# VectorE's order inside a Runge-Kutta stage: operations placed between the two scans that close the stage

## The reference, cut to what matters

```python
def _derivative(q, p, drive, coupling, bias):
    i_couple = jnp.tanh(q) @ coupling.T
    dq = q - q ** 3 / 3.0 - p + drive + i_couple + bias
    dp = EPSILON * (q + ALPHA - BETA * p)
    return (dq, dp)

def _rk4_step(q, p, drive, coupling, bias):
    dq1, dp1 = _derivative(q, p, drive, coupling, bias)
    dq2, dp2 = _derivative(q + 0.5 * DT * dq1, p + 0.5 * DT * dp1, drive, coupling, bias)
    dq3, dp3 = _derivative(q + 0.5 * DT * dq2, p + 0.5 * DT * dp2, drive, coupling, bias)
    dq4, dp4 = _derivative(q + DT * dq3, p + DT * dp3, drive, coupling, bias)
    q_next = q + DT / 6.0 * (dq1 + 2 * dq2 + 2 * dq3 + dq4)
    p_next = p + DT / 6.0 * (dp1 + 2 * dp2 + 2 * dp3 + dp4)
    q_next = jnp.clip(q_next, -CLAMP, CLAMP)
    p_next = jnp.clip(p_next, -CLAMP, CLAMP)
    return (q_next, p_next)
```

## Time and profile before

| what | us |
|---|---|
| median of 3 runs | 5615.42 |
| the profiled execution's own time | 5619.32 |
| its span, first to last instruction | 5617.5 |
| the stretch of the 512 steps in it | 2971.85 |
| VectorE busy in that stretch | 2823.98 |
| TensorE busy in that stretch | 2125.34 |

### The profile page before, as it was taken

One profiled execution on the slowest core, in us unless ns is written; L12 is line 12 of the kernel. 1 busy time (PEld: TensorE's weight loads), 2 busy tenths in 40 slices (PEclk: granted clock), 3 DMA queues, 4 the chain that ended last, 5 costly groups with the idle time before them and its releaser, 6 DMA issues. The chain is left out here.

```text
span 5617.5 us, 214944 instructions
## 1 busy us (share of the span) xinstructions
PE 4455.2 (79%) x79945; PEld 3854.9 (69%) x79945; DVE 4321.5 (77%) x25970; ACT 2307.7 (41%) x10530; POOL 1700.8 (30%) x5981
## 2 busy tenths in 40 slices
PE   6777777777777777777776888599999999969999
PEld 5666666666666666666665666578777787758777
DVE  8999999999999999999996666377777777731123
ACT  3333333333333333333333556255555555432243
POOL 2333333333333333333333322023232323200000
PEclk5555555555555555555556999699999999989999
DMA  1000000000000000000002001222222221131031
GB/s 69 1 1 1 1 1 1 1 1 1 1 1 1 1 1 1 1 1 1 1 1 77 9 24 35 92 65 75 79 94 79 64 94 57 57 120 60 24 112 38
DMA packets 145846, 188.08 MB, mean 33 GB/s; under 512 B 9372, under 2 KB 75492, under 8 KB 145288
## 3 DMA queue, kind: packets, MB, share of 16 engines
q1 hardware_dynamic: 140800, 182.67, 9.7%
q0 software_dynamic: 624, 0.75, 0.1%
q10 hardware_dynamic: 3992, 0.17, 0.0%
HBM read 143.67 MB, written 39.90 MB: 33 GB/s over the span
## 5 line engine op out<-in xcount | busy, mean ns | idle before, releaser
L211 PE MATMUL bank<-tanh_parts,w_lo 128*128 128x4 f16 x32768 | 1208.6, 169 | 845.9 <-ACT tanh_parts L168 845.8
L211 PEld LDWEIGHTS bank<-tanh_parts,w_lo 128*128 128x128 f16 x32768 | 1034.9, 105 | 1029.7 <-ACT tanh_parts L168 1029.2
L168 ACT ACTIVATE tanh_parts<-ys 128x8 f16<-128x8 f32 x4096 | 851.2, 208 | 1902.6 <-DVE ys L306 1902.3
L219 PE MATMUL bank<-tanh_parts,w_hi 128*128 128x8 f16 x32768 | 1206.5, 173 | 1.6 <-issue 1.6
L219 PEld LDWEIGHTS bank<-tanh_parts,w_hi 128*128 128x128 f16 x32768 | 1063.3, 104 | 1.7 <-issue 1.7
L169 ACT ACTIVATE tanh_full<-ys 128x8 f32<-128x8 f32 x4096 | 803.3, 196 | 0.0
L306 DVE TENSOR_TENSOR_SCAN ys<-mix,bank 128x24 f32<-128x24 f32 x4096 | 719.0, 198 | 57.5 <-PE bank L219 3.8
L298 DVE TENSOR_TENSOR tanh_parts<-tanh_full,tanh_parts 128x8 f16<-128x8 f32 x4096 | 689.2, 178 | 0.5 <-ACT tanh_full L169 0.5
L1281 POOL TENSOR_TENSOR t_w_qk<-t_raw_qk,t_w_qk 128x512 fp32r<-128x512 f32 x128 | 168.1, 1335 | 771.4 <-ACT t_w_qk L1445 771.4
L486 PE MATMUL t_bank<-t_x,t_w_qk 128*128 128x512 f32 x1536 | 361.1, 391 | 12.8 <-DVE t_x L1701 12.8
L486 PEld LDWEIGHTS t_bank<-t_x,t_w_qk 128*128 128x128 f32 x1536 | 289.8, 189 | 73.9 <-DVE t_x L1701 13.5
(11 more groups left out here) (238 smaller groups left out, 9545.9 us busy)
## 6 DMA issues: line engine op xcount, KB each, us to landing
t_raw_qk<-L_cond_qkv_w_dram SPq DMA_DIRECT2D x128, 256.0 KB, 3.3
t_raw_vo<-L_cond_qkv_w_dram SPq DMA_DIRECT2D x16, 1024.0 KB, 5.1
t_raw_vo<-L_cond_out_w_dram SPq DMA_DIRECT2D x16, 1024.0 KB, 5.3
n<-t_parts SPq DMA_DIRECT2D x14, 1024.0 KB, 6.6
g_raw<-L_cond_ffn_w_dram SPq DMA_DIRECT2D x8, 1024.0 KB, 9.1
g_x<-n SPq DMA_DIRECT2D x8, 1024.0 KB, 8.6
ada_w<-L_cond_ada_w_dram SPq DMA_DIRECT2D x4, 1536.0 KB, 11.1
t_x<-n SPq DMA_DIRECT2D x6, 1024.0 KB, 7.2
```

What stands on the lines that cost most here:

```text
L168: act.activation(tanh_parts[:, u, at, :, 0], ys[:, s, at, :, 2], ACT.Tanh, scale=1.0 / SCALE).then_inc(s_th, 1)
L211: pe.matmul(sums[:, :, 2], w_lo[:, w_of, k, m * P:(m + 1) * P], tanh_parts[:, u, k, :, 0], start=(m % 2 == 0 and k == 0), stop=False, skip ...
L219: last = pe.matmul(sums[:, :, 1:3], w_hi[:, w_of, k, m * P:(m + 1) * P], tanh_parts[:, u, k], start=False, stop=(m % 2 == 1 and k == C - 1 ...
```

## The change

It does four things, all in VectorE's program:

1. `result` takes a function `between` and runs it between the two scans. In stage 0 the operation `p_1` stands there, in stage 1 the second `known`, in stage 3 the clip of `p`; stage 2 has none.
2. `twice` moves from in front of stage 0's scans to in front of stage 1's. Stage 1's first `known` moves from in front of its `mix` to the stage's start, in front of `cub`. Stage 1's `mix` now stands in front of `p_2`.
3. In stage 0 the first low part stands in front of `cub`.
4. `settle` and the clearing of `s_dve` are gone; the count runs on to the end. With it the loop over steps calls the four stages plainly.

The waits follow: the first scan of stage 0 now waits for `s_mm` and for `s_dve` (the end of `mix`), as stage 3's did and does, and the clip of `p` waits for nothing of its own.

```diff
-            def settle():
-
-                nonlocal n
-                v.wait_ge(s_dve, n)
-                v.sem_clear(s_dve)
-                n = 0
-                marks.clear()
...
-            def result(t, s):
+            def result(t, s, between=None):
...
                                          banks[2 * u + half][:, 0:C // 2 * B * 3], 0.0, ALU.mult, ALU.add).then_inc(s_q, 1)
+                    if half == 0 and between is not None:
+                        between()
...
             def stage_0(t):
...
+                low_part(t, 0, 0)
                 v.wait_ge(s_clip, t + 1)
                 cubed(q[:, :, :])
-                low_part(t, 0, 0)
                 low_part(t, 0, 1)
...
                 based(0, known[:, 0])
-                v.wait_ge(s_rate, t * 3 + 1)
-                own("p_1", stt(ps_[:, 1], rate[:, 0], EPSILON * H, p[:, :, :]))
                 after("base")
-                own("twice", stt(twice[:, :, :], net[:, :, :], 2 * H, q[:, :, :]))
-                result(t, 0)
+
+                def between():
+                    v.wait_ge(s_rate, t * 3 + 1)
+                    own("p_1", stt(ps_[:, 1], rate[:, 0], EPSILON * H, p[:, :, :]))
+                result(t, 0, between)
 
             def stage_1(t):
+                own("known", stt(known[:, 1], rate[:, 0], -EPSILON * H * H, known[:, 0]))
                 v.wait_ge(s_q, t * 2 * STAGES + 4)
...
-                own("known", stt(known[:, 1], rate[:, 0], -EPSILON * H * H, known[:, 0]))
+                after("slope")
+                based(1, known[:, 1])
                 v.wait_ge(s_rate, t * 3 + 2)
                 own("p_2", stt(ps_[:, 2], rate[:, 1], EPSILON * H, p[:, :, :]))
-                after("known")
-                based(1, known[:, 1])
                 v.wait_ge(s_third, t + 1)
                 own("third_1", stt(thirds[:, 1], y1, THIRD, thirds[:, 0]))
                 after("base")
-                own("known", stt(known[:, 2], rate[:, 1], -2 * EPSILON * H * H, twice[:, :, :]))
-                result(t, 1)
+                own("twice", stt(twice[:, :, :], net[:, :, :], 2 * H, q[:, :, :]))
+
+                def between():
+                    after("twice")
+                    own("known", stt(known[:, 2], rate[:, 1], -2 * EPSILON * H * H, twice[:, :, :]))
+                result(t, 1, between)
...
                 based(3, thirds[:, 3])
-                after("moved")
-                v.tensor_scalar(p[:, :, :], p_new[:, :, :], (-CLAMP - SHIFT_P) * SCALE, (CLAMP - SHIFT_P) * SCALE,
-                                ALU.max, ALU.min).then_inc(s_p, 1)
                 after("base")
-                result(t, 3)
-
-            def up_to_stage_2(t):
+
+                def between():
+                    v.tensor_scalar(p[:, :, :], p_new[:, :, :], (-CLAMP - SHIFT_P) * SCALE, (CLAMP - SHIFT_P) * SCALE,
+                                    ALU.max, ALU.min).then_inc(s_p, 1)
+                result(t, 3, between)
...
-                if t + 1 < T:
-                    up_to_stage_2(t + 1)
-                    if t % UNROLL == UNROLL - 1:
-                        settle()
```

More of the change, by code:

```diff
@@ L375, in stage_2 @@
                 own("late", stt(known[:, 3], rate[:, 2], -2 * EPSILON * H * H / 3, thirds[:, 2]))
+                result(t, 2)
             def stage_3(t):
@@ L390, in stage_3 @@
                 based(3, thirds[:, 3])
-                after("moved")
-                v.tensor_scalar(p[:, :, :], p_new[:, :, :], (-CLAMP - SHIFT_P) * SCALE, (CLAMP - SHIFT_P) * SCALE,
-                                ALU.max, ALU.min).then_inc(s_p, 1)
                 after("base")
-                result(t, 3)
-            def up_to_stage_2(t):
+                def between():
+                    v.tensor_scalar(p[:, :, :], p_new[:, :, :], (-CLAMP - SHIFT_P) * SCALE, (CLAMP - SHIFT_P) * SCALE,
+                                    ALU.max, ALU.min).then_inc(s_p, 1)
+                result(t, 3, between)
+            for t in range(T):
                 stage_0(t)
@@ L400, in up_to_stage_2 @@
                 stage_2(t)
-            def from_stage_2(t):
-                result(t, 2)
                 stage_3(t)
[L406 to L409, removed]
-                if t + 1 < T:
-                    up_to_stage_2(t + 1)
-                    if t % UNROLL == UNROLL - 1:
-                        settle()
             v.wait_ge(s_q, T * 2 * STAGES + 2)
```

## The result

The changed kernel takes 5520.49 us, the median of 4 runs (5515.4 to 5520.96); the kernel before took 5615.35 in the same comparison. The forecast was 5567 and the range began at 5520. The direction and the gain in stage 0 were foreseen, and the first rival's time was 5523. The gain in stage 2 was not foreseen: that term had the wrong sign. The size that was forecast, 48 us, is half of what came.

A forecast was written before the change was run, and what follows sets the result against it. VectorE, 95% busy, was taken to start the first scan late, mainly in stage 0. Terms 46 + 15 + 0 - 13 + 0 = 48 us took 5619.3 to 5571, less 3.9 for the median: 5567; range 5520 to 5600.

The forecast's parts named there:

- first rival: Rival A: meetings of VectorE and GpSimd fall the other way; gain 92 us, about 5523, chance 0.22.
- Stage 0's first scan: No longer behind `p_stages` and `twice`, it starts 0.09 us earlier (ends 0.03 and 0.13): 46 us faster (15 to 67).
- The settling: Removing it before stage 2's scans saves 0.12 us net, 127 times: 15 us faster.
- Stage 1: First scan's lateness of 0.03 goes, a late second low part loses 0 to 0.05: 0 (ends -10 and +15 us).
- Stage 2: `rate` and the low part slide by about 0.03, low part still 0.01 behind `gp`: 13 us slower; other end about +16.
- Stage 3: First scan keeps its double wait, matmuls decide it, the later second scan delays nothing: 0, ±12 us.
- Rival A: VectorE first where `cub` and `gq` meet, `mix` meets nothing, one low part gets away: 92 us, about 5523; chance 0.22.
- Rival B: `mix` is pushed, so stage 0 gives only 0.03: 17 us gained, 5598; chance 0.18.
- rival C: An operation behind a scan waits for the scan's end; three stages each lose 0.11 us: slower, 5736; chance 0.06.

The follow-up runs named there:

- stage-0-only kernel: The kernel before with only stage 0's pair changed: first scan directly behind `mix`, `p_stages` between the scans, `twice` behind the second; 5590.35 us, ratio 0.9946.
- experiment with the clip of `p`: The changed kernel with the clip of `p` back in front of stage 3's scans; 5552.13 us, ratio 0.9882.
- experiment with the early `gp`: The changed kernel with GpSimd's first `gp` moved to stage 0, waiting for that stage's `rate`; 5512.56 us, ratio 0.9804.
- experiment with the early copy: The changed kernel with GpSimd copying the next step's drive in stage 1, not stage 3, in three steps of four; 5510.69 us, ratio 0.9804.
- three gains together: The changed kernel with the first `gp` moved to stage 0, the drive copied early and the waits of stage 3's first scan exchanged; 5472.17 us, ratio 0.9742.

## Why the prediction was wrong in size

The bound was read rightly: the first scan was late behind VectorE's own operations, most in stage 0. Against the measured 91.9 us in the stretch the sum had 48. Two of its steps failed, stage 2's term and the end of stage 0's `mix`, and they make up 28 and 20 us of the difference. By its steps:

- **Stage 0's first scan**, forecast 0.09, measured 0.130 us: 20 us too little. The step that failed is "if `mix` ends where it does now". The stage-0-only kernel shows that 0.09 is right for that. The experiment with the clip of `p` shows that the other 0.04 came with GpSimd's chain, which slipped so that `mix` no longer stood behind `thirds`; without the other move, `cub`'s, `mix` stands behind `thirds` again and the matmuls come later besides. The forecast saw both moves and that `cub` and `gq` would fall together, but took a value between the outcomes. Its upper end, 0.13, the matmuls' bound, is what came.
- **The settling**, forecast 15 us: 15.0 by itself. Right.
- **Stage 1**, forecast nothing with the meeting at 0.79: measured -3 us, with the low part at 0.22, within its ends. Right, and the experiment with the early `gp` shows that this meeting holds 0.026 us a step.
- **Stage 2**, forecast -13: the step that failed most. With the settling's own part, the sum had 7 us in this stage (20 less 13), the trace 35. `rate` and the low part slid by 0.03 as forecast, and the meeting took place where it was expected, 0.01 behind `gp`. What failed is that VectorE would pay for it again: GpSimd paid. The high blocks of the first bank took 0.36 instead of 0.40 us, and stage 2 went to 1.353 us in every step instead of to 1.41. That is read from the two traces; no run turned this meeting back alone, and why it fell the other way stays open.
- **Stage 3**, forecast nothing beyond the 5 us given back behind the settling: -6. Right in sum. The meeting with the drive's copy, 9 to 17 us by the experiment with the early copy, was there before the change and was not seen.
- **Rival A** was the outcome, with 0.22: 67 us in stage 0, the settling's 15 and 10 more in stage 2 against the measured 66, 15 and 15, less 3 in stage 1 and 1 in stage 3. Its condition, that the operations fall the other way, was met in stages 0 and 2 and not in stage 1. **Rival B** and **rival C** did not occur: the operation between two scans starts 0.12 behind the first.

The Trainium skill's rule ("SBUF — State Buffer", Who interferes with whom) gave the right pairs, and the trace agrees that the two exclude each other. It says that the second one to issue blocks. By the recorded starts this is not exact, as the last section shows, and the forecast of stage 2 hung on it.

## What to carry to other kernels

Where an engine at 90% busy closes a serial chain, first move what the closing operation does not need behind it; that part can be priced from the rows: stage 0's pair alone came to 0.088 us against 0.09. Then look at every pair of two-input operations of VectorE and GpSimd that start within 0.05 us of one another, since moving anything shifts them, and give GpSimd's operation a wait that puts it beside a scan or a stall. Of two waits on one instruction, write first the one that is satisfied last.

## What the runs showed of the hardware

- VectorE's and GpSimd's operations with SBUF inputs exclude each other, and at starts within some 10 ns the recorded order doesn't tell who pays. Counted over the 13 traces here, 12,274 times, for GpSimd's two `gp` behind a `rate` and VectorE's low part or `slope` that starts nearest: where VectorE's recorded start was from 14 ns in front to 6 ns behind GpSimd's, VectorE's operation was held in 4 of 4423 cases (else 0.16 to 0.18 us), and GpSimd's took 0.25 instead of 0.22; from 7 to 10 ns behind, VectorE's was held in 363 of 2246; from 11 to 40 ns behind, in 5602 of 5605, to about 0.245 us behind GpSimd's start.
- It is not a matter of the recorded distance alone. Of the 363, 357 are in the trace of the kernel before without the settling, and there no case from 7 to 10 ns was free. With the drive's copy and `rate`, 11 to 14 ns apart, VectorE was held in 1419 cases and free in 734. What decides inside this band was not tested.
- A clip, with one input in SBUF, meets GpSimd too: with the three gains together, that of `q` started 13 to 25 ns behind `net` in 486 steps and took 0.22 to 0.24 instead of 0.17 us. A scan, with its second input in PSUM, did not: 2607 scans started 8 to 60 ns behind a GpSimd operation, and none took more than the 0.205 us that scans reach without one.
- A second wait on an instruction is a separate instruction in VectorE's queue. The scan starts 0.035 us behind what its own wait stands for and 0.103 to 0.106 behind what the separate one stands for, whichever is later. So the separate wait costs nothing where it ended early enough (stage 0 with the early clip of `p`: 0.034 behind `mix`, 0.158 behind the bank), and decides even where it ended 0.03 before the other.
- A low part that is late by little costs more than its lateness: in stage 1 of the changed kernel the fifth high block, the first to need it, starts 0.114 us behind the first instead of stage 2's 0.107, and the last starts 0.313 instead of 0.293 behind the fifth (medians). So 0.007 us of waiting cost 0.027; why the blocks behind the wait run longer was not tested.
